# Window attention and a merge convolution on one core: QKV product in two equal halves, another order on ScalarE and GpSimd, another opening and tail

## The reference, cut to what matters

```python
def layer0(x):                      # x after group norm
    v  = einsum('bchw,oc->bohw', x, V_w) + V_b
    qk = einsum('bchw,oc->bohw', x, QK_w) + QK_b
    # windows of 8x8 = 64 tokens, 6 heads of 32 channels
    o = irfft2(rfft2(q) * rfft2(k))            # circular convolution of q and k
    attn = softmax(einsum('bhnd,bhmd->bhnm', o, v) + bias)   # bias: small MLP on positions
    y = einsum('bhnm,bhmd->bhnd', attn, v)
    return einsum('bchw,oc->bohw', y, proj_w) + proj_b

def layer1(x):                      # x after group norm
    out = x + conv3x3(x, laplacian, depthwise)
    return conv1x1(out, merge_w) + merge_b

x = x + layer0(group_norm(x))
x = x + layer1(group_norm(x))
```

## Time and profile before

| | |
|---|---|
| median of 3 runs | 6497.19 us (6494.64 to 6500.95) |
| the profiled execution, its own time | 6496.43 us |
| span of that execution, first to last instruction | 6494.6 us |
| mean granted TensorE clock | 0.992 of full |
| busy: PE, PEld, DVE, ACT, POOL | 96%, 82%, 82%, 56%, 32% |
| share of the chain that ended last: PE, DVE, POOL, ACT | 57%, 24%, 10%, 7% |

### The profile page before, as it was taken

How to read it: one execution, slowest core, us unless ns; L and a number is a source line. 1 busy time by engine, 2 the same in 40 slices (tenths; PEclk the granted TensorE clock), 3 DMA queues, 4 the chain that set the end, 5 groups by cost and what they waited for, 6 DMA issues and landing times.

```text
span 6494.6 us, 222120 instructions
## 1 busy us (share of the span) xinstructions
PE 6218.2 (96%) x95620; PEld 5308.6 (82%) x95620; DVE 5311.9 (82%) x11941; ACT 3663.8 (56%) x9024; POOL 2065.2 (32%) x2310
## 2 busy tenths in 40 slices
PE   7999999999999999999999999999999999999987
PEld 5888788888888888888888888888888888888875
DVE  5777788888888888888888888888888888888878
ACT  3666655555555555555555555555555555555540
POOL 1333333333333333333333333333333333333320
PEclk9999999999999999999999999999999999999999
DMA  3211223223323222322332322332333332232226
GB/s 130 67 61 42 62 75 105 85 65 104 91 85 96 75 83 85 109 75 80 92 96 85 93 77 84 92 104 65 89 94 91 89 81 64 65 86 65 69 73 166
DMA packets 378996, 551.42 MB, mean 85 GB/s; under 512 B 23399, under 2 KB 283562, under 8 KB 365739
## 3 DMA queue, kind: packets, MB, share of 16 engines
q1 hardware_dynamic: 378028, 537.21, 28.7%
HBM read 335.80 MB, written 201.33 MB: 83 GB/s over the span
## 4 chain that ended last, share of the span: by engine, by line
PE 57%; DVE 24%; POOL 10%; ACT 7%; issue 2%; SPq 0%; DMA 0%; DVEq 0%; ACTq 0%
PE b_q L467 13%; PE b_t L516 7%; POOL probs L959 6%; PE b_s L536 5%; PE b_s L429 4%; DVE qkl L812 4%; DVE bn L717 4%; PE b_o L506 4%; ACT probs L916 3%; DVE late L820 3%; DVE ssum L830 3%; PE b_s L496 3%; DVE smax L729 3%; POOL xl L954 3%; ACT qkh L871 3%; PE b_o L405 2%
## 5 line engine op out<-in xcount | busy, mean ns | idle before, releaser
L948 POOL TENSOR_TENSOR probs<-probs,srec 128x384 f32<-128x384 f32 x1024 | 849.3, 829 | 3709.1 <-DVE srec L863 3709.1
L812 DVE TENSOR_TENSOR qkl<-b_q,qkh 128x384 fp32r<-128x384 f32 x1024 | 569.5, 556 | 615.7 <-ACT qkh L871 604.0
L959 POOL TENSOR_TENSOR probs<-probs,smax 128x384 f32<-128x384 f32 x1024 | 907.7, 886 | 415.1 <-DVE smax L729 415.1
L724 DVE TENSOR_TENSOR probs<-b_s,posb 128x384 f32<-128x384 f32 x1024 | 553.3, 540 | 331.6 <-PE b_s L536 330.7
L916 ACT ACTIVATE probs<-probs 128x384 f32<-128x384 f32 x1024 | 535.5, 523 | 481.0 <-POOL probs L959 480.3
L467 PE MATMUL b_q<-wnh,xh 128*128 128x192 f32 (+1 forms) x2048 | 790.7, 386 | 3.2 <-DVE xhl L834 2.7
L871 ACT ACTIVATE probsT<-b_s 128x384 f32<-128x384 f32 x1024 | 502.8, 491 | 503.2 <-PE b_s L429 503.2
L871 ACT ACTIVATE qh<-b_t 94x384 f32<-94x384 f32 x1024 | 497.8, 486 | 465.5 <-PE b_t L516 465.5
L536 PEld LDWEIGHTS b_s<-vT,osb 32*64 32x64 f32 x24576 | 450.2, 132 | 286.1 <-ACT osb L871 205.5
L871 ACT ACTIVATE yT<-b_s 128x256 f32<-128x256 f32 x1024 | 392.7, 384 | 460.7 <-PE b_s L496 459.1
L820 DVE SCALAR_TENSOR_TENSOR late<-b_s,pb,xs 128x128 f32<-128x128 f32 (+1 forms) x2048 | 610.5, 340 | 27.5 <-PE b_s L486 5.7
(11 more groups left out here) (154 smaller groups left out, 15129.2 us busy)
## 6 DMA issues: line engine op xcount, KB each, us to landing
ld<-in_x SPq DMA_DIRECT2D x96, 1024.0 KB, 4.9
late<-x_dram SPq DMA_DIRECT2D x112, 640.0 KB, 6.2
xs<-in_x SPq DMA_DIRECT2D x128, 512.0 KB, 5.6
x_dram<-late SPq DMA_DIRECT2D x128, 512.0 KB, 2.8
out<-late SPq DMA_DIRECT2D x128, 512.0 KB, 4.6
late<-x_dram SPq DMA_DIRECT2D x240, 192.0 KB, 6.6
xs<-in_x SPq DMA_DIRECT2D x128, 256.0 KB, 6.2
x_dram<-late SPq DMA_DIRECT2D x128, 256.0 KB, 3.6
```

The source lines that it names most:

```text
L812: V.tensor_tensor(qkl[:, :], q_out, qkh[:, :].bitcast(F32), ALU.subtract).then_inc(lo_out, 1)
L948: P.tensor_tensor(probs[:, i % 3, :, :], probs[:, i % 3, :, :], srec[:, i % 2, :].unsqueeze(2).broadcast_to([128, 6, N]), ALU.mult).then_i ...
L959: P.tensor_tensor(probs[:, i % 3, :, :], probs[:, i % 3, :, :], smax[:, i % 2, :].unsqueeze(2).broadcast_to([128, 6, N]), ALU.subtract).th ...
```

## The change

Six edits:

1. The QKV product is cut in two halves of 288 columns, columns 288 to 575 first (the last 96 of k, then v), then 0 to 287. In PSUM the 576 columns stand around the border of the two banks of `b_q`.
2. The transposed v goes to the unused columns 384 to 511 of the two banks of `b_t`. So the transposes wait for `prod_done` of the pair before (DVE's L733 reads `b_t`), L516 waits for `vT_out` of its own pair, and the wait for `vT_out` ahead of the QKV product goes.
3. On ACT `qkh` and `vT` are copied ahead of the exponential.
4. On POOL the subtraction of the maximum comes ahead of `xl`.
5. In the tail, pieces 0 to 3 get the source added by a third float32 matmul with the identity, and ACT writes the result with the bias; DVE keeps pieces 4 and 5. A semaphore `a_read` counts what ACT has read.
6. In the opening the four group norm steps are put into the loop over the positions, at m = 8, 16, 40 and 52.

```diff
-        q_out, v_psum, vt_out = b_q[:, 0:QK], b_q[:, 512:512 + C], b_q[:, 512 + C:512 + C + 256]
+        first = 512 - QKV // 2
+        q_out, v_psum = b_q[:, first:first + QK], b_q[:, first + QK:first + QKV]
+        vt_out = b_t.rearrange("p (t c) -> p t c", t=2)[:, :, QK:512]
...
             for m in range(N):
+                if m == 8:
+                    group_mean(0)
+                elif m == 16:
+                    group_spread(0)
+                elif m == 40:
+                    bias(0, 0)
+                elif m == 52:
+                    pe.wait_ge(m_read, 3)
+                    bias(0, 1)
...
                 if p < 4:
                     mm(o, mats(par, 0), za[:, k, p * 256:(p + 1) * 256], start=True, stop=False)
                     at = p % 2 * 256
-                    mm(o, mats(par, 3 + p // 2), zb[:, k, at:at + 256], start=False, stop=True).then_inc(m_mm, 1)
+                    last = mm(o, mats(par, 3 + p // 2), zb[:, k, at:at + 256], start=False, stop=not alone)
+                    if alone:
+                        last = mm(o.rearrange("p (r c) -> p r c", c=W), ident[:, :],
+                                  src_a[v % 3][:, 2 * p + 1:2 * p + 3, 1:W + 1], start=False, stop=True)
+                    last.then_inc(m_mm, 1)
...
-                    if pair(1):
-                        pe.wait_ge(vT_out, n - 1)
...
-                    for o, lo, up, done in ((v_psum, QK, QKV, v_mm), (q_out, 0, QK, qkv_mm)):
+                    for lo, up, done in ((QKV // 2, QKV, v_mm), (0, QKV // 2, qkv_mm)):
+                        o = b_q[:, first + lo:first + up]
                         for k, (xx, ww, t) in enumerate(products):
                             last = mm(o, xx[:, h % 2, at], ww[:, par, t, lo:up], start=(k == 0), stop=(k == 4))
                         last.then_inc(done, 1)
                     pe.wait_ge(v_out, n)
+                    if pair(1):
+                        pe.wait_ge(prod_done, n - 1)
...
                     pe.wait_ge(lo_out, n)
+                    pe.wait_ge(vT_out, n)
...
                     if kind == "piece":
-                        dve.wait_ge(m_mm, m_count[it])
-                        result(at, p, it)
+                        if it < ALONE or p >= 4:
+                            dve.wait_ge(m_mm, m_count[it])
+                            result(at, p, it)
...
+                if it >= ALONE and task and task[0] == "piece" and task[2] < 4:
+                    _, v, p = task
+                    if p == 0:
+                        act.wait_ge(out_sent[v % 2], 48 * (v // 2))
+                    act.wait_ge(m_mm, m_count[it])
+                    A.activation(res_a[:, v % 2, p * 256:(p + 1) * 256], m_region(it)[:, 0:256], ACT.Identity,
+                                 bias=mc[:, v // NS % 2, 0:1]).then_inc(a_read, 1)
...
+                if pair(0):
+                    i, n = pair(0)
+                    act.wait_ge(qkv_mm, n)
+                    copy(qkh[:, :], q_out).then_inc(hi_out, 1)
+                    act.wait_ge(vT_mm, n)
+                    copy(vT[:, i % 2, :, :], vt_out).then_inc(vT_out, 1)
                 if pair(2):
                     i, n = pair(2)
                     act.wait_ge(sub_done, n)
                     pr = probs[:, i % 3, :, :].rearrange("p s m -> p (s m)")
                     A.activation(pr, pr, ACT.Exp).then_inc(exp_done, 1)
```

More of the change, by code:

```diff
@@ L222, in program, with m_wait @@
         iterations = range(-4, 8 * BLOCKS)
-        m_count, used = {-5: 4}, 4
+        ALONE = PAIRS + 2 * 8
+        m_count, d_count, a_count = {-5: 4}, {-5: 4}, {-5: 0}
         for it in iterations:
-            used += m_task(it) is not None
-            m_count[it] = used
-        ALONE = PAIRS + 2 * 8
+            by_act = it >= ALONE and it % 8 < 4
+            m_count[it] = m_count[it - 1] + (m_task(it) is not None)
+            d_count[it] = d_count[it - 1] + (m_task(it) is not None and not by_act)
+            a_count[it] = a_count[it - 1] + (m_task(it) is not None and by_act)
         def m_region(it):
             return b_q[:, 0:256] if it >= ALONE and it % 2 else b_o[:, 192:512]
-        def m_free(it):
-            return m_count[it - 2] if it > ALONE else m_count[it - 1]
+        def m_wait(eng, it):
+            eng.wait_ge(m_read, d_count[it])
+            if a_count[it]:
+                eng.wait_ge(a_read, a_count[it])
         def pairs():
@@ L354, in _, with group_mean, group_spread, bias @@
             pe.wait_ge(hid_relu, 2 * (N * N // 512))
-            for m in range(N):
+            m_out = m_region(0)
+            def group_mean(b):
+                pe.wait_ge(g1_aggr, b + 1)
+                mm(m_out[:, 0:1], part_mates[:, :], gst[:, 0:1], start=True, stop=True).then_inc(m_mm, 1)
+            def group_spread(b):
+                pe.wait_ge(g1_dev, b + 1)
+                if b == 0:
+                    pe.wait_ge(m_read, 1)
+                mm(m_out[:, 0:2], part_spread[:, 0:CA], gst[:, 0:2], start=True, stop=True)
+                mm(m_out[:, 2:4], part_spread[:, CA:256], gst[:, 0:2], start=True, stop=True).then_inc(m_mm, 1)
+            def bias(b, part):
+                pe.wait_ge(norm0_w, b + 1)
+                lo, up = part * QKV // 2, (part + 1) * QKV // 2
+                o = m_out[:, 0:QKV // 2]
+                mm(o, ones[0:1, :], qkvb[:, lo:up], start=True, stop=False)
+                mm(o, negmean[:, 0, :], wn[:, 0, lo:up], start=False, stop=False)
+                mm(o, negmean[0:CB, 1, :], wn[0:CB, 1, lo:up], start=False, stop=True).then_inc(m_mm, 1)
+            for m in range(N):
+                if m == 8:
[7 more added lines that the diff above has]
+                    bias(0, 1)
                 for t in range(2):
@@ L401, in piece @@
                 par, k, o = v // NS % 2, v % 2, m_region(it)[:, 0:256]
+                alone = it >= ALONE
                 if p == 0:
@@ L412, in piece @@
                     mm(o, mats(par, 5), zb[:, k, at:at + 256], start=False, stop=True).then_inc(m_mm, 1)
-            group_mean(0)
-            group_spread(0)
-            for part in range(2):
-                pe.wait_ge(m_read, 2 + part)
-                bias(0, part)
             pe.wait_ge(m_read, 4)
@@ L502, in _ @@
                     if task:
[L503 removed]
+                        pe.wait_ge(m_read, d_count[it])
                     for k in range(3):
@@ L916, in _ @@
                     A.activation(pr, pr, ACT.Exp).then_inc(exp_done, 1)
-                if pair(0):
-                    i, n = pair(0)
-                    act.wait_ge(qkv_mm, n)
-                    copy(qkh[:, :], q_out).then_inc(hi_out, 1)
-                    act.wait_ge(vT_mm, n)
-                    copy(vT[:, i % 2, :, :].rearrange("p t m -> p (t m)"), vt_out).then_inc(vT_out, 1)
                 if pair(4):
@@ L961, in _ @@
                                     ALU.subtract).then_inc(sub_done, 1)
+                h = (it + 4) // 4
+                if it % 4 == 2 and 0 <= h < PAIRS // 4:
+                    pool.wait_ge(xh_done, 3 * h + 2)
+                    P.tensor_tensor(tokens(xl, 0, h), windows(0, h), tokens(xh, 0, h).bitcast(F32), ALU.subtract
+                                    ).then_inc(xl_done, 1)
 def kernel(**inputs):
```

34 lines of the change are left out of this document (7 added, 27 removed).

## The result

| | before | after |
|---|---|---|
| median, runs side by side | 6497.39 us (6494.64 to 6500.95) | 6341.66 us (6337.45 to 6342.56) |
| ratio, 95% interval | | 0.9758 (0.9742 to 0.9773) |
| profiled execution, its span | 6496.43, 6494.6 us | 6342.08, 6340.3 us |

A forecast was written before the change was run, and what follows sets the result against it. PE's rate bounds phases 1 to 5 and 7; phases 6 and 0 wait through POOL, ACT and DVE. 175 steady + 49 before layer 1 + 10 opening - 10 tail = 224 us off, 6273 us; range 6205 to 6385.

The forecast's parts named there:

- the halves bring nothing: Rival, QKV product: time grows straight with columns, or the next wait takes the gain; 6343 us, chance 13%.
- POOL and DVE collide: Rival, phase 6: DVE held up by half a `xl`, 63 us lost, 6336 us; chance 8%.
- The halves: QKV product: 288-column matmuls 0.133 us apart, 0.10 us per pair gained with a piece, 0.05 us in phases 6 and 7.
- ACT's order: Softmax: `qkh` starts when the second half is done; with POOL's order, 0.8 to 0.9 us off phase 6, 0.22 off phase 0.
- The exponential as the late one: Rival, ACT: its 0.3 us margin before DVE's sum is used up; 6529 us at worst, likelier about 6430; chance 5%.
- POOL's order: Softmax: counted with ACT's order as one step, 0.8 to 0.9 us off phase 6; `xl` has room.
- The wait for `prod_done`: Ahead of v's transposes on PE: costs nothing in phases 0 to 5, part of the 0.05 us in phases 6 and 7.
- The stretch before layer 1: 128 pairs before layer 1: 0.42 us per pair above PE's floor shrink to about 0.04, saving 49 us.
- wrong if the transposes wait for `prod` in most phases: Sign in the profile after, at PE's transposes of v, that would show the forecast wrong.
- Opening: Group norm steps inside the position loop: first QKV matmul near 88 us instead of 98.23, 10 us earlier.
- Tail: Last 16 blocks: 10.4 us each at full clock, 3 to 25 us lost, taken as 10 us.
- the prediction's tenth off for image borders: Steady blocks: DVE's group norm chains pace some iterations at image borders, so 195 us saved is cut to 175.

The follow-up runs named there:

- split_before: Changed kernel with the QKV product again in 192 and 384 columns, in the PSUM banks of before; 6402.32 us, ratio 0.9857 to the kernel before.
- act_alone: Kernel before with only ACT's new order, `qkh` and `vT` copied ahead of the exponential; 6342.99 us, ratio 0.9756.
- pool_before: Changed kernel with POOL's old order, `xl` ahead of the subtraction of the maximum; 6283.34 us, ratio 0.9674 to the kernel before.
- prod_wait: Kernel before with ACT's new order and the transposed v in `b_t`, with its two new waits; 6360.38 us, ratio 0.9786.
- late_transposes: Changed kernel with POOL's old order, v's transposes and their waits behind the projection, exponential between `qkh` and `vT`; 6239.78 us, ratio 0.9599.
- experiment 10: The run `late_transposes`: changed kernel with POOL's old order, v's transposes behind the projection, exponential between `qkh` and `vT`; 6239.78 us, ratio 0.9599.
- pieces_reordered: Kernel of `late_transposes` with DVE's pieces 4 and 5 first in the tail, ACT's four behind them; 6214.16 us, ratio 0.9559.
- late_and_tail: Kernel of `late_transposes` with the tail undone: DVE writes all six results, no third matmul; 6228.13 us, ratio 0.9581.

## Why the prediction came out as it did

The time lies in the range 6205 to 6385, 69 us above the forecast and outside the forecast's own 6230 to 6315. It is within 6 us of what two rivals gave, "the halves bring nothing" (6343) and "POOL and DVE collide" (6336). `split_before` rules out the first (the halves are worth 61 us), and the second was right in its mechanism alone. Step by step:

- **The halves: right.** 0.1325 us for a forecast 0.133, and 61 us for a forecast 66 (0.10 us in six phases of 110 blocks). The missing sixth phase is phase 2. The gain of 0.05 us that I gave to each of phases 6 and 7 did not come: `split_before` has 5.18 us in both as well, and phase 7 went up from 5.12 to 5.18.
- **ACT's order: right, and the largest term.** Phase 6 came to 5.17 us (forecast 5.15), and phase 0 gained about what was said. By the runs it is worth 125 us inside the change and about 155 alone; I had 106 us for ACT's and POOL's order together and a part of the 49 us before layer 1. The exponential as the late one, a rival, did not come: DVE's sum waited 9.1 us in all for it.
- **POOL's order: the step that failed.** The forecast took "ACT and POOL in the new order" as one step that removes 0.8 to 0.9 us in phase 6. ACT's half alone does that: `act_alone` has 5.17 us there, with `xl` still first. POOL's half costs 58 us. I had priced the rival in phase 6 (63 us, with 8%); the mechanism and nearly the size were right, the place was not. `xl` is made in phase 2 too, and there DVE has L704 and L688 ahead of `qkl`. In phase 6 there is no L688; POOL's subtraction of the maximum is the one that is slow (1.67 us), `xl` begins at 3389.23, behind `qkl`, and PE's L534 waits for nothing. I had read one phase with `xl`, and not the other. `pool_before` is at 6283.34 us, 10 us from the forecast; that is luck in part, since it has the same 27 us missing before layer 1 and makes up for 17 of them elsewhere.
- **The wait for `prod_done`: undersized.** "It costs nothing" in phase 0, and nothing before layer 1. `prod_wait` shows 17 us for edit 2, 15 of them before layer 1 and by its start times the wait for the product. In the steady stretch phase 0 has none, as forecast, and phases 6 and 7 have it where the forecast put it: in the kernel after, the transposes begin 0.31 us after the start of the last QKV matmul in these two phases and 0.13 us after it in the others. Before layer 1 they begin 0.15 us after the product's end in all eight phases, which is the sign "wrong if the transposes wait for `prod` in most phases" for that stretch.
- **The stretch before layer 1: half missed.** Forecast 49 us, measured (44.62 - 43.24) x 16 = 22 us. `act_alone` reaches (44.62 - 42.41) x 16 = 35 us, and `prod_wait` with edit 2 falls back to 23, so the wait for the product takes 13 us of it. `late_transposes` gets 60 us by moving the transposes. The rest of the forecast's gap, 14 us, is there without that wait too: the weight loads of PE also wait for `vs` and `osb` there, and my 0.04 us of rest per pair had no row for that.
- **Opening: right** (10.8 us in the trace, 9.7 by a run of its own; forecast 10). **Tail: right** (7 us lost; forecast 10). The block is 10.44 us at full clock for 10.4, and the half-clock stretches became fewer instead of staying.

In sum: the collision's 58 us and the 27 us missing before layer 1 make 85; the tail cost 3 us less than forecast, and the rest of the steady stretch, which is what is left over, brought 14 us more. That makes the 68 us between 224 and 156; the prediction's tenth off for image borders lies in those 14 and was not tested by itself. The single runs added up (155 + 61 + 10 - 17 - 7 - 58 = 144 us) miss the measured 156 by 12; which edits overlap there was not tried.

Three of the prediction's own sums are off, none in the forecast's main sum: 0.10 us in six phases of 110 blocks is 66 us and not 70; half of the 256 us of the late exponential gives 6401 us and not 6430; and 11 us for a tail block against 10.25 makes 12 us lost in 16 blocks, so the upper end of 25 us has no working.

Of what "the profile after will show": spacing, phase 6, the opening and the tail held. The pairs from 200 to 800 us, "L516 without waits on `qkl`", and "no wait of `qkl` on `qkh` over 0.3 us" did not. The waits of the kernel after from 1000 to 6000 us:

```profile
DVE qkl L831 <- ACT qkh L890: 109.9, 223, 1.3
...
PE b_t L534 <- DVE qkl L831: 62.3, 123, 1.4
```

PE's waits lie in phase 2 once in each of the 105 blocks of this window. The waits of `qkl` for `qkh` have a mean of 0.49 us and lie mostly in phases 5 to 7, where PE then does not wait.

## What to carry to other kernels

When a change moves an operation that runs in several phases, lay out every phase in which it runs, and look at what stands beside it on the other engines in each. Take an order on two engines apart into one edit for each engine: here one half gave the whole gain and the other took a third of it back, and alone that other half measured as nothing, because a loss and a gain cancelled. Put the copy that another engine and PE wait for ahead of the work whose reader is far away (155 us here), and put a new wait behind all matmuls that don't need it (experiment 10, of which this is a part, gained 44 us).

## What the hardware showed that was not expected

**POOL and DVE took turns by whole instructions.** In phase 2 of the kernel after, L704 ran from 3363.63 to 3364.32. `xl` began beside it at 3363.73 and ended at 3365.45; from the end of L704 that is 1.13 us of its usual 1.28. L688 began at 3364.24, and after the end of `xl` it had 0.68 us of its usual 0.82 left. So each stood still for most of the time that the other ran. The Trainium skill ("SBUF — State Buffer", Who interferes with whom) says that a DVE instruction with two inputs in SBUF and a POOL instruction that reads SBUF lock each other out for their whole length; the trace agrees, with 1.89 us for 0.82. What it cost was decided by the place: 1.07 us of DVE's time became 0.44 us of the iteration.

**288 columns of float32r start 0.1325 us apart**, 0.013 us more than 288 columns at 2.4 GHz. Plain float32 of the same width starts 0.345 us apart, instruction by instruction, so a time read for one type says little of the other.

**The granted clock in the tail was higher with the third matmul.** It was 0.96 to 0.98 over the 16 blocks in the six kernels that have it in the order of the change, 1.00 in `pieces_reordered`, and 0.90 to 0.93 in the seven without it, `before` among them. `late_and_tail` and `late_transposes` differ in edit 5 alone: 0.93 and 0.98. PE has 576 matmul instructions in these blocks instead of 448. Edit 5 also moves four results to ACT, so that it is the matmuls is likely and not parted from the rest.
